# Gated delta attention with adaLN: triangular inverse built on 32 instead of 64 columns a unit, its dense factor transposed by VectorE and ScalarE instead of TensorE

## The chip, the cores and the metric

The kernel runs on one core of one Trainium2 chip, as one program. The metric is the device time of that core in microseconds. Before the change the median of 3 runs is 5353.44 us (5352.12 to 5354.04).

## The reference, cut to what matters

The whole computation is an adaLN block on x of 8 samples x 512 tokens x 256 channels: layer norm with modulation, a gated delta rule attention with 16 key heads and 32 value heads of width 128, a second layer norm, and a mixture of 2 of 6 small experts. Nearly all of the time lies in the attention, and the change lies in one part of it, the inverse of a unit lower triangular matrix:

```python
qkvz = hidden_states @ W_qkvz.T          # then a causal convolution of 4 taps and silu on q, k, v
q, k = l2norm(q) * dk ** -0.5, l2norm(k)
g = cumsum(g, chunk);  decay = tril(exp(g_i - g_j))
A = -strict_tril((k * beta) @ k.T * decay)          # one matrix for each head and chunk
T = solve_triangular(eye - A, eye, lower=True)      # the inverse of (I - A)
value_, k_cumdecay = T @ v_beta, T @ (k_beta * exp(g))
# then chunk by chunk, with a carried state:
v_new = value_ - k_cumdecay @ state
out   = (q * exp(g)) @ state + tril(q @ k.T * decay) @ v_new
state = state * exp(g_last) + (k * exp(g_last - g)).T @ v_new
```

The reference cuts the 512 tokens into chunks of 64; the kernel uses chunks of 128, which is the same recurrence. So one step of the kernel inverts 8 matrices of 128x128 ("units": 4 chunks x 2 value heads).

## The kernel before, in words

Three programs follow one another: `modulation_and_gates` (about the first 105 us), `attention`, and `experts` (about the last 170 us). `attention` walks over 128 steps, 8 samples x 16 key heads. A step works on one key head of one sample and its two value heads.

**How the order is fixed.** Each engine has its own list of tasks for one iteration (`PE_ORDER`, `ACT_ORDER`, `DVE_ORDER`, `POOL_ORDER`). A task is written `NAMEn@k`: the task NAME, its part n, of the step that lies k steps ahead of the iteration's own number. So an iteration works on up to four steps at once. Each engine executes its list strictly in that order; tasks of different engines are tied by semaphores, counted for each step (`counts`, and `t.wait(engine, name, k, back)`, where `back=1` means the step before). The loop body holds two iterations. SyncE issues the loads with its own list, `FEEDS`: pairs of a load and the number of steps that it runs ahead. A load whose wait is not met holds up all that stand behind it in the list.

**The tasks that matter here.**

- `P` (TensorE, 12 of them): the input projection, in two PSUM banks; `C` (ScalarE): its results copied and scaled; `T` (VectorE, 12): the taps of the convolution; `Z`, `SV`, `SQ`, `SK` (ScalarE): silu. `KT`, `QT`, `VT` transpose k, q, v on TensorE.
- `KK` (TensorE): k.T k and k.T q. `GL` (GpSimd), `GE` (ScalarE, behind a table load): the decay matrix `dec`. `GA` (VectorE, 8 instructions): `ga`, the scaled and decayed product. `SL` (GpSimd): its diagonal set to -1. `AD` (ScalarE): `a_d`, `ga` rounded to bf16. `AL` (GpSimd): the rest of the rounding, `a_lo`.
- The inverse by levels, in bf16, in one PSUM bank `p_lev` of 8 units x 64 columns. `AB` (VectorE): the two 64x64 diagonal blocks of each unit of `a_d` are copied into `a_bd`. `L` (TensorE): `a_bd` times an identity. `y0` (VectorE): the result times a mask. Then for n = 1 to 5: `M` (TensorE, `a_bd` times `y_h`), `q` (VectorE, times the level's mask, to `q_h`), `X` (VectorE, `y_h` transposed in 32x32 blocks to `x_t`), `XB` (ScalarE, the blocks of `x_t` copied to `x_bd`), `Y` (TensorE, `x_bd` times `q_h`), `y` (VectorE, added to `y_h`). Each of `L`, `M`, `Y` is 8 matmuls. After level 5 the 64x64 blocks are inverted.
- The join to 128: `s10`, `s11` (VectorE) copy `y_h` to the diagonal blocks of `y_dn`, the dense factor. `XD` (TensorE) transposes `y_dn` with 8 transpositions into `p_tr`, and `XD` (ScalarE) copies that to `x_dn`. `Q`, `p`, `Z`, `YC` (TensorE, VectorE, TensorE, ScalarE) make the lower left 64x64 block, `XC` (TensorE and ScalarE) its transpose.
- Two correction passes in higher precision: `D`, `d`, `N`, `n`, `E`, `e`, `W`, `IV` give `inv_t`.
- The recurrence over the 4 chunks: `TR`, `VW`, `U`, `ST`, `KS`, `RR`, `O`, `VX`, `SD`, `QD` (GpSimd, q times its decay, which `O1` to `O3` need). Then `OT`, `OQ`, `OS`, `OP`, `ON`, `HT`, `OY`, `YA`: the norm of the output and the output projection.

Where the tasks of one engine stand decides what waits. In the list of before GpSimd runs `GL@3 SL@2 SD1@1 QD@2`, ScalarE ends its list with `KT@3 XD@2 KN@3 YC@2 d0@2 d1@2 XC@2 GE@3` and begins it with `Z0@2 Z1@2 e0@1 IV0@1 AD@2 VX0@1`. VectorE begins with `VW0@1 AB0@2 AB1@2`. `FEEDS` begins with the weights, 3 steps ahead.

At the start of `attention`, GpSimd raises every semaphore by 3 steps' counts, clears `a_bd`, `x_bd`, `y_dn`, `pre` and `y_acc` and makes the small constants; the other engines wait for it (`init`).

Of the kernel before, what the change touches and what calls it, by code (L numbers as in the profile page):

```python
# [33 lines left out]
PE_ORDER = ("Z6@1 P9@2 D0@1 XC@1 D1@1 ON0@0 N0@1 ON1@0 P10@2 N1@1 KK0@2 KK1@2 P11@2 E0@1 P0@3 W0@1 E1@1 TR0@1 "  # L34
            "P1@3 U0@1 O0@1 L@2 W1@1 KS1@1 P2@3 M1@2 TR1@1 Y1@2 U1@1 O1@1 M2@2 P3@3 KS2@1 VT0@2 Y2@2 VT1@2 TR2@1 "
            "P4@3 M3@2 P5@3 U2@1 Y3@2 O2@1 M4@2 OY0@0 KS3@1 P6@3 Y4@2 TR3@1 QT@3 M5@2 O3@1 P7@3 Y5@2 P8@3 Q6@2 "
            "KT@3 XD@2 OY1@0")
ACT_ORDER = ("Z0@2 Z1@2 e0@1 IV0@1 AD@2 VX0@1 e1@1 SV1@2 OT0@1 C0@3 XB1@2 SV0@2 VX1@1 XB2@2 IV1@1 OT1@1 C1@3 OQ0@1 "
             "XB3@2 VX2@1 VK0@2 C2@3 VK1@2 OT2@1 XB4@2 OQ1@1 SQ@3 VX3@1 OQ2@1 XB5@2 OT3@1 OQ3@1 SK@3 QN@3 C3@3 "
             "KT@3 XD@2 KN@3 YC@2 d0@2 d1@2 XC@2 GE@3")  # L40
DVE_ORDER = ("VW0@1 AB0@2 AB1@2 T8@2 ST0@1 y0@2 X1@2 RR1@1 q1@2 VW1@1 y1@2 X2@2 ST1@1 q2@2 RR2@1 y2@2 X3@2 VW2@1 "
# [1566 lines left out]
```

## Time and profile before

| | |
|---|---|
| median of 3 runs | 5353.44 us |
| the profiled execution, its own time | 5352.04 us |
| its span in the trace | 5350.3 us |
| busy: TensorE matmul, weight load | 4982.9 us (93%), 3326.6 us (62%) |
| busy: VectorE, ScalarE, GpSimd | 4483.8 us (84%), 4371.8 us (82%), 2064.9 us (39%) |
| DMA queue of SyncE | 21.8% of 16 engines' span |
| mean granted TensorE clock | 0.987 of full |

The trace is one execution, recorded by the hardware. PE is TensorE's matmuls, PEld its weight loads (they overlap), DVE is VectorE, ACT ScalarE, POOL GpSimd, SP SyncE. Each line of a view names the line of the kernel (L911), the instruction, the tile that it writes, those that it reads, and shapes as partitions x elements. A start and a duration are in microseconds. In brackets stands how long the engine sat idle before, and who ended that. An engine's duration includes filling and draining, so the next instruction can start before the last has ended: the distance between two starts is the cost on the engine, the duration is what a reader of the result waits for.

### The profile page before, as it was taken

Reading aid. Unit: us, or ns where it says so; the run is one execution under the profiler, and the core shown is the slowest. Engines: PE = TensorE matmul, PEld = TensorE weight load, DVE = VectorE, ACT = ScalarE, POOL = GpSimd, SP = SyncE. Lnnn points to the kernel's source line nnn. Section 1 sums busy time; section 2 is a strip of 40 time slices with the busy share of each in tenths; the row PEclk is TensorE's granted clock in tenths of the full one; section 3 lists DMA queues with packets and bytes.
Section 4 is the critical chain, followed back from the end, with each engine's and each line's share of the span. In section 5 each row is a group of like instructions: output and inputs, shape, how many; then the busy total and the mean of one; then the engine's idle time right before and its main releaser. Section 6 shows DMA issues by size and latency. Waiting matters only on the chain. (4 is left out here: it accounts for less than half of the span.)

```text
span 5350.3 us, 132947 instructions
## 1 busy us (share of the span) xinstructions
PE 4982.9 (93%) x38788; PEld 3326.6 (62%) x38788; DVE 4483.8 (84%) x9152; ACT 4371.8 (82%) x9744; POOL 2064.9 (39%) x1433
## 2 busy tenths in 40 slices
PE   5899999999999999999999999999999999999978
PEld 3566666666666666666666666666666666666644
DVE  4888888888888888888888888888888888888853
ACT  3788888888888888888888888888888888888842
POOL 2344434344443434444344444434444343444410
PEclk7999999999999999999999999999999999999988
DMA  3222212121121212212121221212122121221112
GB/s 141 75 63 63 75 62 81 60 70 69 62 81 60 79 60 72 71 62 77 60 82 61 65 74 62 81 59 74 65 66 77 60 79 60 72 70 62 64 65 82
DMA packets 185165, 377.26 MB, mean 71 GB/s; under 512 B 86400, under 2 KB 95744, under 8 KB 184960
## 3 DMA queue, kind: packets, MB, share of 16 engines
q1 hardware_dynamic: 185088, 376.46, 21.8%
q14 instruction: 57, 0.47, 0.0%
q8 instruction: 20, 0.33, 0.0%
HBM read 360.13 MB, written 16.25 MB: 70 GB/s over the span
## 5 line engine op out<-in xcount | busy, mean ns | idle before, releaser
L653 PE MATMUL p_proj<-hid,w_in 128*128 128x512 f32 x3072 | 1620.5, 610 | 32.4 <-POOL ident L1163 29.7
L998 DVE SCALAR_TENSOR_TENSOR conv<-pre,taps,conv 128x512 f32<-128x512 f32 x1536 | 1207.8, 793 | 41.9 <-ACT conv L857 37.6
L911 ACT ACTIVATE x_bd<-x_t 64x512 bf16<-64x512 bf16 x1280 | 804.5, 629 | 215.7 <-DVE x_t L1079 198.9
L1205 POOL TENSOR_TENSOR o_sc<-o_sc,neg_half 128x8 f32<-128x8 f32 x128 | 268.6, 2099 | 1622.0 <-DVE o_sc L1135 1622.0
L653 PEld LDWEIGHTS p_proj<-hid,w_in 128*128 128x128 f32 x3072 | 496.6, 192 | 64.5 <-POOL ident L1163 30.0
L838 PE MATMUL p_out<-h_t,w_out 128*128 128x512 f32 x1024 | 501.9, 613 | 0.8 <-DVE h_t L1140 0.8
L1072 DVE TENSOR_TENSOR y_h<-p_lev,y_h 128x512 bf16<-128x512 f32 x640 | 441.3, 690 | 44.2 <-PE p_lev L707 37.9
L1116 DVE TENSOR_TENSOR vw<-p_b,w_c 128x256 f32<-128x256 f32 x384 | 156.9, 409 | 378.8 <-PE p_b L796 378.8
L1079 DVE STREAM_TRANSPOSE x_t<-y_h 128x512 bf16<-128x512 bf16 x640 | 454.6, 710 | 19.3
L1064 DVE TENSOR_TENSOR q_h<-p_lev,consts 128x512 bf16<-128x512 f32 x640 | 438.6, 685 | 37.9 <-PE p_lev L701 33.3
L1172 POOL TENSOR_TENSOR low<-g_row,consts 128x1024 f32<-128x1024 f32 x128 | 302.1, 2360 | 410.1 <-ACT dec L895 409.9
L1200 POOL TENSOR_TENSOR state_dec<-state,g_exp 128x256 f32<-128x256 f32 x256 | 157.3, 615 | 764.5 <-DVE state L1123 501.9
L1051 DVE SCALAR_TENSOR_TENSOR ga<-p_out,neg_c,dec 128x256 f32<-128x256 f32 x1024 | 413.0, 476 | 23.3 <-PE p_out L677 15.3
L818 PE MATMUL p_b<-vx,ga 128*128 128x128 f32 x2048 | 374.8, 275 | 0.0
L707 PEld LDWEIGHTS p_lev<-q_h,x_bd 128*128 128x128 bf16 x5120 | 219.4, 98 | 240.1 <-ACT x_bd L911 176.4
L857 ACT ACTIVATE conv<-p_proj,taps 128x512 f32<-128x512 f32 x512 | 353.2, 690 | 1.6
L856 ACT ACTIVATE pre<-p_proj 128x512 f32<-128x512 f32 x512 | 305.5, 597 | 32.1 <-PE p_proj L653 32.0
L817 PE MATMUL p_b<-state,q_dec 128*128 128x128 f32 x1536 | 324.0, 293 | 0.5 <-ACT vx L960 0.5
L1193 POOL TENSOR_TENSOR q_dec<-kq,e_row 128x512 f32<-128x512 f32 x256 | 320.5, 1274 | 0.0
L701 PEld LDWEIGHTS p_lev<-y_h,a_bd 128*128 128x128 bf16 x5120 | 223.3, 98 | 156.1 <-issue 144.3
L895 ACT ACTIVATE dec<-low,g_neg 128x128 f32<-128x128 f32 x1024 | 313.2, 388 | 1.5
L1105 DVE SCALAR_TENSOR_TENSOR rr<-p_a,g_exp,v_tok 128x128 f32<-128x128 f32 x768 | 228.3, 339 | 101.6 <-PE p_a L783 101.6
(210 smaller groups left out, 12168.4 us busy)
## 6 DMA issues: line engine op xcount, KB each, us to landing
w_in<-in_w_in SPq DMA_DIRECT2D x128, 768.0 KB, 6.2
g_row<-rows_scratch SPq DMA_DIRECT2D x128, 512.0 KB, 3.1
hid<-h_scratch SPq DMA_DIRECT2D x128, 512.0 KB, 7.3
e_row<-exp_rows_scratch SPq DMA_DIRECT2D x128, 512.0 KB, 5.1
w_out<-in_w_out SPq DMA_DIRECT2D x128, 256.5 KB, 2.6
x<-in_x SPq DMA_DIRECT2D x8, 512.0 KB, 10.4
h_scratch<-x SPq DMA_DIRECT2D x8, 512.0 KB, 2.6
y_scratch<-y_acc SPq DMA_DIRECT2D x8, 512.0 KB, 5.6
```

The lines of the kernel that those rows point to most:

```text
L653: last = pe.matmul(p_proj[tile % 2][:], w_in[p][:, kt, tile * P:(tile + 1) * P], hid[p][:, kt, :], start=(kt == 0), stop=(kt == KT - 1))
L817: pe.matmul(p_b[:, at], q_dec[p][:, n, h, :], state[n % 2][:, h, :], start=True, stop=False)
L818: last = pe.matmul(p_b[:, at], ga[p][:, n * HD + h, 1, :], vx[:, h, :], start=(n == 0), stop=True)
L838: last = pe.matmul(p_out[n][:], w_out[p][:, h * D + n * P:h * D + (n + 1) * P], h_t[:, :, h, :], start=(h == 0), stop=(h == HD - 1))
L857: act.activation(conv[:, n, :], p_proj[n % 2][:], ACT.Copy, scale=taps[p][:, n, PAD:PAD + 1])\
L911: last = act.activation(x_bd[block, :, block], x_t[block], ACT.Copy)
L998: dve.scalar_tensor_tensor(conv[:, tile, :], pre[:, tile, j:j + S], taps[p][:, tile, j:j + 1], conv[:, tile, :], ALU.mult, ALU.add).then_i ...
L1051: last = dve.scalar_tensor_tensor(ga[p][:, u], kk, neg_c[p][:, n, h:h + 1], each(dec[:, u, :], 2), ALU.mult, ALU.mult)
L1064: dve.tensor_tensor(q_h[:], levels(), each(const["mask"][:, n * HB:(n + 1) * HB], U), ALU.mult)\
L1072: dve.tensor_tensor(y_h[:], levels(), y_h[:], ALU.add).then_inc(s["y_done"], 1)
L1079: dve.transpose(x_t[:].rearrange("p u f -> p (u f)"), y_h[:].rearrange("p u f -> p (u f)"))\
L1193: last = pool.tensor_tensor(q_dec[p][:, :, h, :], kq[p][:, :, 1, :], e_row[p][:].rearrange("p (c h) i -> p c h i", h=HD)[:, :, h, :], ALU. ...
```

## The change

The levels run on 32 columns a unit: the four 32x32 diagonal blocks of each unit are inverted by levels, so `p_lev` is used on 8 x 32 columns, and the masked levels are one fewer. The join from 32 to 64 is the last `M`/`Y` pair, with the off-diagonal blocks `a_off` in place of `a_bd` and no mask. The dense factor's transpose no longer passes through TensorE: its diagonal 32x32 blocks are copied by ScalarE from `x_t` (which `X5` made), the two off-diagonal blocks are transposed by VectorE (`XE`). The lists of all engines and `FEEDS` are new, and so is the start of `attention`.

```diff
-LEVELS = 6
+LEVELS = 5
+PE_ORDER = ("P11@2 E0@1 P0@3 W0@1 E1@1 TR0@1 P1@3 U0@1 P2@3 L@2 O0@1 KS1@1 M1@2 P3@3 TR1@1 W1@1 Y1@2 P4@3 M2@2 "
+            "U1@1 O1@1 Y2@2 P5@3 KS2@1 P6@3 VT0@2 M3@2 TR2@1 VT1@2 Y3@2 U2@1 O2@1 M4@2 P7@3 KS3@1 Y4@2 OY0@0 M5@2 "
+            "TR3@1 P8@3 QT@3 Y5@2 O3@1 KT@3 Q6@2 OY1@0 Z6@2 P9@3 XC@2 D0@2 D1@2 P10@3 ON0@1 ON1@1 N0@2 N1@2 KK0@3 "
+            "KK1@3")
+ACT_ORDER = ("Z0@2 SV1@2 Z1@2 e0@1 IV0@1 AD@2 VX0@1 e1@1 C0@3 OT0@1 XB1@2 C1@3 OQ0@1 VX1@1 XB2@2 IV1@1 SV0@2 OT1@1 "
+             "C2@3 XB3@2 OQ1@1 VX2@1 VK0@2 XB4@2 VK1@2 SQ@3 OT2@1 SK@3 XB5@2 VX3@1 C3@3 OQ2@1 QN@3 OT3@1 OQ3@1 "
+             "XD@2 KN@3 YC@2 KT@3 d0@2 XC@2 d1@2 GE@3")
+DVE_ORDER = ("HT0@0 HT1@0 SM0@2 n0@1 SM1@2 SM2@2 SM3@2 n1@1 GA0@2 GA1@2 GA2@2 GA3@2 T7@2 T8@2 VW0@1 AB0@2 AB1@2 "
+             "AB2@2 AB3@2 ST0@1 y0@2 X1@2 RR1@1 q1@2 VW1@1 y1@2 X2@2 T3@3 AB4@2 q2@2 T0@3 ST1@1 y2@2 T4@3 X3@2 "
+             "RR2@1 SN1@2 T1@3 q3@2 VW2@1 y3@2 X4@2 T5@3 ST2@1 q4@2 T2@3 RR3@1 y4@2 AB5@2 X5@2 T6@3 YA0@0 q5@2 "
+             "s8@2 s9@2 s10@2 s11@2 YD0@2 SN0@2 XE0@2 YD1@2 XE1@2 OS0@1 OS1@1 p6@2 SN2@2 T9@3 T10@3 YA1@0 KN@3 "
+             "QN@3 T11@3")
+POOL_ORDER = ("OP@0 ON@0 PW@2 GL@3 QD@1 SL@2 SD1@1 AL@2 SD2@1")
...
-            FEEDS = ((weights, 3), (gate_cols, 3), (out_weights, 1), (gate_exps, 1), (rows, 4),
-                     (tap_rows, 3), (gate_rows, 3))
+            FEEDS = ((gate_cols, 3), (weights, 3), (tap_rows, 3), (rows, 3), (gate_exps, 1),
+                     (gate_rows, 1), (out_weights, 0))
...
                 elif name == "M":
                     t.wait(pe, "y_done", n)
+                    if n == 5:
+                        t.wait(pe, "abd")
+                    rows = a_off if n == 5 else a_bd
                     for u in range(U):
-                        last = pe.matmul(p_lev[:, u * HB:(u + 1) * HB], a_bd[:, u, :], y_h[:, u, :], start=True, stop=True)
+                        last = pe.matmul(p_lev[:, u * QB:(u + 1) * QB], rows[:, u, :], y_h[:, u, :], start=True, stop=True)
...
-                elif name == "XD":
-                    t.wait(pe, "ydn")
-                    t.wait(pe, "x12", back=1)
-                    for u in range(U):
-                        last = pe.transpose(p_tr_h[:, u * P:(u + 1) * P], y_dn[:, u, :], ident_h[:])
-                    last.then_inc(s["xt6"], 1)
...
-                    for block in (slice(0, HB), slice(HB, P)):
-                        last = act.activation(x_bd[block, :, block], x_t[block], ACT.Copy)
+                    for block in range(4):
+                        last = act.activation(x_bd[part(block), :, part(block)], x_t[part(block)], ACT.Copy)
...
                 elif name == "XD":
-                    t.wait(act, "xt6")
+                    t.wait(act, "xt_done")
                     t.wait(act, "w_mm", back=1)
-                    act.activation(x_dn[:].rearrange("p u i -> p (u i)"), p_tr_h, ACT.Copy).then_inc(s["xdn"], 1)
+                    for block in range(4):
+                        last = act.activation(x_dn[part(block), :, part(block)], x_t[part(block)], ACT.Copy)
+                    last.then_inc(s["xdn"], 1)
...
-                    dve.tensor_copy(a_bd[half(n), :, half(n)], a_d[half(n), :, half(n)]).then_inc(s["abd"], 1)
+                    if n < 4:
+                        dve.tensor_copy(a_bd[part(n), :, part(n)], a_d[part(n), :, part(n)]).then_inc(s["abd"], 1)
+                    else:
+                        j, i = part((n - 4) * 2), part((n - 4) * 2 + 1)
+                        dve.tensor_copy(a_off[j, :, i], a_d[j, :, i]).then_inc(s["abd"], 1)
...
+                elif name == "YD":
+                    t.wait(dve, "y_mm", 5)
+                    i, j = part(n * 2 + 1), part(n * 2)
+                    dve.tensor_copy(y_dn[i, :, j], levels()[i]).then_inc(s["ydn"], 1)
+                elif name == "XE":
+                    t.wait(dve, "ydn", 5 + n)
+                    i, j = part(n * 2 + 1), part(n * 2)
+                    dve.transpose(x_dn[j, :, i], y_dn[i, :, j]).then_inc(s["xe"], 1)
...
-            for name, counted in s.items():
-                pool.sem_inc(counted, SPARE * counts[name])
-            for tile in (a_bd, x_bd, y_dn):
-                pool.memset(tile[:], 0.0)
+            spare(pool, "rooted g_low strict alo q_dec_done sdec opow o_nrm")
```

`part(n)` is the n-th slice of 32 (`QB`), `HB` is 64. `s8` to `s11` copy the four diagonal blocks into `y_dn`, in place of two copies; `y5` is gone, `YD0` and `YD1` take its result straight from `p_lev`. `spare` raises the semaphores that an engine signals on that engine itself; VectorE now clears the tiles (`a_off` and `x_dn` among them) and of `pre` only the padding; and TensorE's first projection no longer waits for `init`, only `L` of the first step does. `Q` reads `y_dn` in place of `y_h`.

## Rows read from the trace of the kernel before

**Rows 1.** Windows, steady stretch: length, busy of PE, PEld, DVE, ACT, POOL, clock, DMA, GB/s.

```profile
2000.00:3000.00 1000.00, 951.57 (x7604) 639.83 (x7603) 870.56 (x1795) 855.79 (x1921) 408.45 (x281) 1.00 0.22 68
```

**Rows 2.** GpSimd's `OP`, one a step: count, durations (ns), first and last start.

```profile
L1205 POOL TENSOR_TENSOR o_sc<-o_sc,neg_half x125: 2082/2106/2109, 249.4 to 5095.8; 128x8 f32<-128x8 f32 x125
```

**Rows 3.** Waits of ScalarE, window 2000:4000: us in total, times, longest.

```profile
ACT x_bd L911 <- DVE x_t L1079: 76.1, 102, 1.3
ACT f L947 <- PE p_out L750: 67.7, 102, 1.1
ACT inv_t L943 <- PE p_out L778: 49.7, 51, 1.0
```

**Rows 4.** Timeline of TensorE: start, us, what, idle before.

```profile
3005.54 0.40 PE L701 MATMUL p_lev<-y_h,a_bd 128*128 128x64 bf16 x8
3005.77 0.69 PE L796 MATMUL p_b<-rr,inv_t 128*128 128x128 f32 x4
...
3024.25 0.61 PE L713 MATMUL p_tr<-ident_h,y_dn 128*128 128x128 bf16 x8
3024.70 1.94 PE L838 MATMUL p_out<-h_t,w_out 128*128 128x512 f32 x4
...
3031.28 0.40 PE L760 MATMUL p_out<-f,x_dn 128*128 128x128 bf16 x4 [1.15 <-DVE h_t L1140]
```

**Rows 5.** Groups of instructions, all of the span: count, busy us, mean ns, idle before.

```profile
L911 ACT ACTIVATE x_bd<-x_t 64x512 bf16<-64x512 bf16 x1280 | 804.5, 629 | 215.7 <-DVE x_t L1079 198.9
...
L1079 DVE STREAM_TRANSPOSE x_t<-y_h 128x512 bf16<-128x512 bf16 x640 | 454.6, 710 | 19.3
L1072 DVE TENSOR_TENSOR y_h<-p_lev,y_h 128x512 bf16<-128x512 f32 x640 | 441.3, 690 | 44.2 <-PE p_lev L707 37.9
...
L1057 DVE COPY a_bd<-a_d 64x512 bf16<-64x512 bf16 x256 | 73.4, 287 | 6.4 <-ACT a_d L903 2.4
...
L1123 DVE COPY state<-p_a 128x256 f32<-128x256 f32 x128 | 53.4, 418 | 0.8 <-PE p_a L806 0.8
```

**Rows 6.** Timeline of ScalarE, one iteration.

```profile
3005.21 1.27 ACT L911 ACTIVATE x_bd<-x_t 64x512 bf16<-64x512 bf16 x2 [0.21 <-DVE x_t L1079]
3006.50 0.63 ACT L878 ACTIVATE v_t<-conv 128x512 f32<-128x512 f32 x1
...
3025.50 1.04 ACT L916 ACTIVATE x_dn<-p_tr 128x1024 bf16<-128x1024 bf16 x1
3026.40 0.62 ACT L882 ACTIVATE squares<-p_out 128x512 f32<-128x512 f32 x1
3027.08 0.59 ACT L922 ACTIVATE y_dn<-p_lev 64x512 bf16<-64x512 f32 x1
...
3029.69 0.60 ACT L947 ACTIVATE f<-p_out 128x512 bf16<-128x512 f32 x1 [0.32 <-PE p_out L750]
...
3032.07 2.44 ACT L895 ACTIVATE dec<-low,g_neg 128x128 f32<-128x128 f32 x8
...
3039.81 1.05 ACT L903 ACTIVATE a_d<-ga 128x1024 bf16<-128x1024 f32 x1
...
3044.72 1.27 ACT L911 ACTIVATE x_bd<-x_t 64x512 bf16<-64x512 bf16 x2 [0.35 <-DVE x_t L1079]
```

**Rows 7.** Timeline of GpSimd.

```profile
3004.48 2.51 POOL L1193 TENSOR_TENSOR q_dec<-kq,e_row 128x512 f32<-128x512 f32 x2
...
3034.66 2.36 POOL L1172 TENSOR_TENSOR low<-g_row,consts 128x1024 f32<-128x1024 f32 x1 [3.27 <-ACT dec L895]
3038.11 1.10 POOL L1181 TENSOR_SCALAR_AFFINE_SELECT ga<-ga 128x1024 f32<-128x1024 f32 x1 [1.09 <-DVE ga L1051]
```

**Rows 8.** DMA issues on the page: count, KB each, us to landing.

```profile
hid<-h_scratch SPq DMA_DIRECT2D x128, 512.0 KB, 7.3
```

**Rows 9.** Timeline of the start of attention.

```profile
111.28 0.95 POOL L1156 MEMSET a_bd<- 128x1024 bf16 x1 [46.24 <-issue]
...
117.81 8.51 PE L653 MATMUL p_proj<-hid,w_in 128*128 128x512 f32 x14 [29.73 <-POOL ident L1163]
```

More of the change, by code:

```diff
@@ L33 @@
 PAD = TAPS - 1
[L34 to L41, printed above, removed]
[3 rows of a table removed]
-POOL_ORDER = ("OP@0 ON@0 PW@2 GL@3 SL@2 SD1@1 QD@2 SD2@1 AL@2")
+PE_ORDER = ("P11@2 E0@1 P0@3 W0@1 E1@1 TR0@1 P1@3 U0@1 P2@3 L@2 O0@1 KS1@1 M1@2 P3@3 TR1@1 W1@1 Y1@2 P4@3 M2@2 "
[6 more added lines that the diff above has]
+DVE_ORDER = ("HT0@0 HT1@0 SM0@2 n0@1 SM1@2 SM2@2 SM3@2 n1@1 GA0@2 GA1@2 GA2@2 GA3@2 T7@2 T8@2 VW0@1 AB0@2 AB1@2 "
[4 rows of a table added]
+POOL_ORDER = ("OP@0 ON@0 PW@2 GL@3 QD@1 SL@2 SD1@1 AL@2 SD2@1")
 def const_columns():
-    return [("ident", P), ("mean", P), ("ones", P), ("tri", P), ("bound", CH), ("eye", HB), ("mask", LEVELS * HB),
+    return [("ident", P), ("mean", P), ("ones", P), ("tri", P), ("bound", CH), ("eye", QB), ("mask", LEVELS * QB),
             ("upper", P), ("lower", P)]
@@ L692, in emit @@
                 elif name == "L":
-                    t.wait(pe, "abd")
+                    if isinstance(t.number, int) and t.number == 0:
+                        pe.wait_ge(init, 2)
+                    t.wait(pe, "abd", 4)
                     t.wait(pe, "y21", back=1)
                     for u in range(U):
-                        last = pe.matmul(p_lev[:, u * HB:(u + 1) * HB], a_bd[:, u, :], eye_h[:], start=True, stop=True)
+                        last = pe.matmul(p_lev[:, u * QB:(u + 1) * QB], a_bd[:, u, :], eye_h[:], start=True, stop=True)
                     last.then_inc(s["q_mm"], 1)
@@ L719, in emit @@
                     for u in range(U):
-                        last = pe.matmul(p_lev[HB:P, u * HB:(u + 1) * HB], a_d[0:HB, u, HB:P], y_h[0:HB, u, :],
+                        last = pe.matmul(p_lev[HB:P, u * HB:(u + 1) * HB], a_d[0:HB, u, HB:P], y_dn[0:HB, u, 0:HB],
                                          start=True, stop=True)
@@ L732, in emit @@
                     t.wait(pe, "y21")
-                    t.wait(pe, "xdn")
+                    t.wait(pe, "x12", back=1)
                     pe.sem_inc(passed, 1)
@@ L981, in _ @@
         def _(dve):
[L982 to L985 removed]
+            for tile in (a_bd, a_off, x_bd, y_dn, x_dn, y_acc):
+                dve.memset(tile[:], 0.0)
+            dve.memset(pre[:, :, 0:PAD], 0.0).then_inc(init, 1)
+            spare(dve, "tap0 tap1 tap2 tap3 xe k_sum q_sum scaled w_scaled q_scaled ga_done abd q_done y_done xt_done ydn p6_done "
+                       "n_done rr_done vw_done st_done osm h_done y_added")
+            dve.wait_ge(init, 2)
             def levels():
[L988 removed]
+                return p_lev[:, 0:U * QB].rearrange("p (u f) -> p u f", f=QB)
             def emit(name, t, n):
@@ L1076, in emit @@
                         t.wait(dve, "xbd", back=1)
+                        t.wait(dve, "xdn", back=1)
                     else:
```

70 lines of the change are left out of this document (41 added, 29 removed), and 3 rows, old and new, of the table DVE_ORDER.

## The prediction

> **What bounds the kernel now.** I read the windows first. In the steady stretch of 1000 us TensorE's matmuls are busy 951.6 us, VectorE 870.6, ScalarE 855.8, GpSimd 408.5, at the full clock (1.00, the 2.4 GHz level), and DMA takes 22% [rows 1]. The reader is to see three engines within a tenth of each other: none can be called the bound by its share alone. Next, one task that occurs once a step gives the period: 125 starts of `OP` from 249.4 to 5095.8 us, so (5095.8 - 249.4) / 124 = 39.08 us [rows 2]. In units of one period TensorE is busy 37.2 us, VectorE 34.0, ScalarE 33.5. Some 126 steps run at this pace; the rest is the two other stages, filling and draining.
>
> Then the waits and the timelines, for what each engine's idle time hangs on. TensorE's longest gap is `N0`, 1.15 us behind `HT0` [rows 4], and `HT0` stands behind taps in VectorE's list: in that part VectorE runs without a gap, so VectorE is what binds there. ScalarE idles 5.6 us a period; the two largest pieces are `XB` waiting for the transpose `X` (76.1 us over 51 periods, 1.5 us each) and `d` waiting for `D` (1.3 us), then `IV0` for `W0` (1.0 us) [rows 3]. So the kernel now is bound by a loop over engines in which VectorE has the least slack, TensorE little, and ScalarE 5.6 us. What matters is who gives work and who gets it.
>
> **The change, part by part, for one step.**
>
> *TensorE.* The eight transpositions go: from 3024.25 to the next start at 3024.70, 0.45 us [rows 4]. The levels stay 11 tasks of 8 matmuls. One such task of 64 columns takes 3005.77 - 3005.54 = 0.23 us, 29 ns a matmul, each with its own weight load of 128 columns. With 32 columns I bound it by half (0.12 us a task, 1.2 us a step) and by no gain; each matmul still loads all its weights, so I take no gain. A new wait arises where `ON0`, `ON1`, `N0`, `N1`, `KK0` now follow each other. TensorE needs 36.7 us.
>
> *VectorE.* Work on `p_lev` halves from 512 to 256 elements: 0.69 us becomes 0.42, the duration of the 128x256 copy out of PSUM [rows 5]. That is 10 such instructions (5 `q`, `y0` to `y4`), -2.7 us; `y5` goes, -0.7. `X` scales in the same way, 0.71 to 0.44, five of them, -1.35. Against this: six `AB` copies for two and four `s` copies for two. Two of 64x512 take 0.29 us each plus a gap of 0.03; a block of half the elements I put at 0.24, so +1.2. `YD` twice 0.45, `XE` twice 0.47: +1.85. In sum -1.7 us: VectorE goes from 34.0 to 32.3 us, and `T7`, `T8` (1.4 us) move into its idle time before `VW0`. VectorE is relieved.
>
> *ScalarE.* It pays. `XB` is 2 instructions of 64x512 at 0.629 us [rows 5]; the pair starts at 3005.21 and the next instruction at 3006.50, so it costs 1.29 us, no overlap at either seam [rows 6]. An element costs (1.05 - 0.63) / 512 = 0.82 ns, from the 1024 element copy `AD` and the 512 element silu in the same rows, so 256 elements save 0.21 us and one 32x256 copy takes 0.42, with the gap 0.44. Bounds: 0.32, if it overlaps its successor by 0.10 as 128-partition instructions do (`x_dn` lasts 1.04 us, its successor starts 0.90 after it [rows 6]), and 0.63, if a block cost as much as a larger one. I take 0.44, since the nearest rows are those of the same copy on part of the partitions. `XB`: 5 x (4 x 0.44 - 1.29) = +2.35 us. `XD`: 4 x 0.44 = 1.76 for 0.90, +0.86. ScalarE gets +3.2 us: 33.5 becomes 36.7 of 39.1, and only 2.4 us may be left for all its waits if the period is to stay. Its list is now the tightest loop, so I walk it.
>
> - *From `XB1` to `YC`.* Now 3027.08 - 3005.21 = 21.9 us [rows 6]. Add 3.2; `KT` (0.5) moves behind `YC`; the wait of `XB2` (1.3 of the 1.5) goes, because the level chain gets shorter (`y` and `X` -0.27 each) and more work stands between the `XB`; of small waits I take off another 0.7. 22.6 us.
> - *From `YC` to `d1`.* Now 2.61 us (3027.08 to 3029.69). `XC`, on 64 partitions as `YC` with its 0.59, moves between `d0` and `d1`, +0.6; `d1` no longer idles, -0.32; on TensorE `XC` goes ahead of `D0`, which I put at +0.15. `KT` fills a part of the wait for `D0` and costs nothing. 3.05 us.
> - *From `d1` to the next `XB1`.* Now 15.0 (3029.69 to 3044.72). `d1`, table load and `GE` take 4.2 (`XC` stood between and is gone). Then GpSimd: `GL` cannot start before `GE` is done (its own `low` is read until then) and takes 2.36. Behind it now stands `QD@1`, 2.51 us, ahead of `SL@2`, 1.10 [rows 7]. With hand-overs 6.3, so `AD` starts 10.5 after `d1`. `AD` 1.05, four `AB` 1.0, `L` 0.6, `y0` 0.45, `X1` 0.5 with hand-overs of 0.05: 14.15 us.
>
> 22.6 + 3.05 + 14.15 = 39.8; hand-overs may be a tenth too generous, so I take 39.7 for 39.08: +0.62 us x 126 = +78 us. In this walk `QD` before `SL` costs about 0.9 us of it: `IV0` would be done 9.6 after `d1`, and `AD` waits, with `VX0`, `e1` and `C0` queued behind it on ScalarE, for which `VW1`, `W1` and `T0` wait in turn.
>
> The Trainium skill ("ScalarE: Activation LUTs", section "What ACT_TABLE_LOAD costs") says that back-to-back ACTIVATEs overlap by about 93 ns. By that rule the four copies would cost what two cost now. This case agrees for 128 partitions (0.90 between starts of 1.04) and does not for 64 (1.29 for two of 0.63).
>
> *The loads.* All nine loads of a step now stand behind `gate_cols`, which waits for `SN0` in the last fifth of VectorE's list. The weights land 7.3 us after issue [rows 8]; I estimate some 12 us of listed work between `SN0` and `P0`, and some 13 until `QD` needs `e_row`. Hidden, but no longer by much: cost 0, or up to 1 us a step if late.
>
> *The start.* GpSimd's first clearing is at 111.28 and the first projection at 117.81 [rows 9]. These 6.5 us, which TensorE waited for, go; what gates it next is the landing of its first loads. Between -6.5 and 0 I take -4 us.
>
> **The sum.** 5352.0 (the profiled execution's own time, 1.7 over its span) + 78 - 4 = 5426; the median of runs is 1.4 above that execution: 5427 us.
>
> **Rivals.**
>
> *Copies on 32 partitions overlap.* Then a copy costs 0.32, `XB` nothing more than now, ScalarE's loop falls by 24 x 0.12 = 2.9 to 36.8, and TensorE binds: 36.7 us plus the waits around `N` and `KK`, about 37.8 in all. -1.3 x 126 - 4 = -168: 5185. For it: 128-partition instructions overlap; against it: no 64-partition one does. It decides below a seam of about 0.41 us a copy.
>
> *VectorE was the bound, and ScalarE's waits give way.* My walk keeps 2.9 us of waits on ScalarE. If `QD` ran in a gap before `GL`'s release, or `IV0` and `d0` waited half as long because VectorE arrives earlier, the period would be 38.7: -0.4 x 126 - 4 = -54: 5299. For it: the 1.15 us at `N0` and VectorE's gapless part; against it: these waits hang on TensorE and GpSimd, which get no shorter.
>
> *Gain and cost cancel*: within 0.1 us a step, 5350.
>
> *The loads come late.* One trigger for 2.5 MB; if `P0` or `QD` waited 1 us each step on top of the forecast: 5427 + 126 = 5550. Against it: 22% DMA share.
>
> *The narrower levels do nothing on TensorE*: that is in the forecast already; its other end is -1.2 us of TensorE's work, which pays only if TensorE binds.
>
> **Chances.** About 0.2% (10 us) is what a measurement of this kernel can tell from no change. Forecast 0.50 (its own range 5370 to 5490); overlap 0.10; waits give way 0.26; cancel 0.06; loads late 0.08. Slower 0.58, faster 0.36, same 0.06. The range 5235 to 5500 leaves out most of the overlap case and of the late loads.
>
> **What would show it.** Busy time of ScalarE in a steady window from 856 to about 920 per 1000; `x_bd` near 0.42 us with 0.44 between starts; a period near 39.7; `a_d` waiting about 0.9 us for GpSimd's `ga`; `x_bd`'s waits near zero; VectorE's share falling to about 815, TensorE's matmuls to about 925. The forecast is wrong if the seam between 32-partition copies is below 0.4, or if ScalarE's waits sum to less than 2.4 us a step, or if the first wait of `P0` is a DMA.

## The result: 5909 us for a forecast of 5427

The changed kernel takes 5909.0 us (median of 4 runs, 5908.1 to 5913.1) beside 5352.9 us for the kernel before: a ratio of 1.104, 95% interval 1.1021 to 1.1059. The sign was forecast as likelier than not; the size was not: 5909 lies far above the range 5235 to 5500.

### The profile after

The steady stretch of [rows 1], in the same columns:

```profile
2000.00:3000.00 1000.00, 883.58 (x6655) 579.42 (x6655) 791.62 (x1813) 825.86 (x2013) 367.71 (x253) 0.95 0.18 62
```

Every engine is less busy than before, ScalarE too, and the granted clock has fallen from 1.00 to 0.95 of full speed. Nothing got fuller: there is a new hole. Over a full 90 periods a step took 43.72 us for 39.09 (starts of `a_d`), and not evenly: steps alternate between 41.8 and 45.6 us. A loop turn holds two steps, so the hole comes once a turn. The waits, window 2000:4000 (us in total, times, longest), name it:

```profile
ACT z_t L876 <- PE p_proj L665: 141.5, 23, 7.1
...
PEld p_out L773 <- issue: 100.5, 92, 4.5
```

23 times in 46 steps ScalarE's `z_t` waits for a projection, 6.2 us on average and 7.1 at most; before, no wait of ScalarE was over 1.3 us [rows 3]. The timelines of one such place, VectorE first (start, duration, what, idle before):

```profile
3006.79 0.87 DVE L1015 SCALAR_TENSOR_TENSOR conv<-pre,taps,conv 128x512 f32<-128x512 f32 x1
3010.93 1.41 DVE L1178 SCALAR_TENSOR_TENSOR h_t<-p_out,norm_w,z_t 128x512 f32<-128x512 f32 x2 [3.27 <-issue]
3012.26 2.09 DVE L1030 TENSOR_SCALAR neg_n<-root 128x8 f32<-128x8 f32 x1
...
3015.67 1.12 DVE L1042 SCALAR_TENSOR_TENSOR neg_c<-cc,inv 128x8 f32<-128x8 f32 x1
3016.71 0.68 DVE L1131 SCALAR_TENSOR_TENSOR y<-y_dn,p_out 128x512 f32<-128x512 bf16 x1
3017.50 1.66 DVE L1068 SCALAR_TENSOR_TENSOR ga<-p_out,neg_c,dec 128x256 f32<-128x256 f32 x4
```

then TensorE and ScalarE:

```profile
3011.83 1.24 PE L773 MATMUL p_out<-f,x_dn 128*128 128x128 bf16 x8 [2.99 <-DVE h_t L1178]
3015.08 2.04 PE L689 MATMUL p_out<-kq 128*128 128x256 f32 x4 [2.01 <-DVE y L1131]
3017.53 2.05 PE L689 MATMUL p_out<-kq 128*128 128x256 f32 x4 [0.41 <-DVE y L1131]
```

```profile
3013.14 0.60 ACT L876 ACTIVATE z_t<-p_proj 128x512 f32<-128x512 f32 x1
3013.63 0.62 ACT L892 ACTIVATE v_t<-conv 128x512 f32<-128x512 f32 x1
3021.32 0.60 ACT L876 ACTIVATE z_t<-p_proj 128x512 f32<-128x512 f32 x1 [7.07 <-PE p_proj L665]
```

`T11` is the last entry of the new VectorE list and `HT0` its first: the idle time stands exactly at the branch back. It is put down to "issue", that is, to nothing that a semaphore shows, and small instructions behind it (`neg_n` over 8 columns, 2.09 us) are slow as well. TensorE waits 2.99 us for `HT0` and then 2.01 for `y`, and the windows of that stretch show its clock (third-last column the granted clock, then the DMA share):

```profile
3005.00:3010.00 5.00, 3.76 (x35) 2.41 (x34) 2.66 (x4) 4.05 (x8) 3.94 (x2) 1.00 0.94 338
3010.00:3014.00 4.00, 1.17 (x8) 0.69 (x8) 3.07 (x3) 3.97 (x10) 2.03 (x1) 0.66 0.27 111
3014.00:3020.00 6.00, 4.51 (x9) 3.02 (x10) 5.18 (x11) 0.26 (x1) 2.76 (x3) 0.50 0.00 1
```

Behind the idle time the clock is 0.50, the 1.2 GHz level, and four matmuls of `KK` take 2.04 us. `P11` stands behind `KK` in TensorE's list, hence the 7.07 us of ScalarE.

The cause shows in the page's list of DMA queues (packets, MB, share). The kernel before has 57 packets on queue 14; after:

```profile
q14 instruction: 364, 2.98, 0.2%
```

These packets of 8192 bytes carry instructions. Over the whole loop they come 5.6 a turn, before 0.6. So part of some engine's loop is loaded anew in each turn, which I call a refetch. The queue does not say for which engine; the idle time at VectorE's branch points to VectorE, and experiment 5, which changes VectorE's program alone, confirms it. Which bodies are loaded anew, and what it costs, had to be found.

### The profile page after: what moved, and what is told of

Same layout as the page of the kernel before. It is cut to its first block and busy times, and to the rows that moved or that the text cites. A ratio compares the mean times of both kernels' runs of the same rounds, so it can differ in the third digit from the quotient of the medians.

```text
span 5911.3 us, 135338 instructions
## 1 busy us (share of the span) xinstructions
PE 5151.8 (87%) x37764; PEld 3349.3 (57%) x37764; DVE 4553.1 (77%) x10311; ACT 4703.8 (80%) x11408; POOL 2067.7 (35%) x1428
## 5 line engine op out<-in xcount | busy, mean ns | idle before, releaser
L665 PE MATMUL p_proj<-hid,w_in 128*128 128x512 f32 x3072 | 1682.4, 631 | 25.8 <-DMA hid<-h_scratch 23.1
L925 ACT ACTIVATE x_bd<-x_t 32x256 bf16<-32x256 bf16 x2560 | 1053.2, 411 | 48.0 <-DVE x_t L1104 16.0
L1238 POOL TENSOR_TENSOR o_sc<-o_sc,neg_half 128x8 f32<-128x8 f32 x128 | 210.9, 1648 | 1901.0 <-DVE o_sc L1173 1901.0
L689 PE MATMUL p_out<-kq 128*128 128x256 f32 x1024 | 387.0, 515 | 149.1 <-DVE y L1131 146.9
L876 ACT ACTIVATE z_t<-p_proj 128x512 f32<-128x512 f32 x256 | 152.4, 595 | 375.2 <-PE p_proj L665 370.8
L689 PEld LDWEIGHTS p_out<-kq 128*128 128x128 f32 x1024 | 228.3, 247 | 265.5 <-issue 237.9
L1178 DVE SCALAR_TENSOR_TENSOR h_t<-p_out,norm_w,z_t 128x512 f32<-128x512 f32 x256 | 180.6, 747 | 244.8 <-issue 174.6
L783 PEld LDWEIGHTS p_out<-y,ga 128*128 128x128 f32 x2048 | 279.1, 207 | 122.5 <-issue 119.8
L1096 DVE TENSOR_TENSOR y_h<-p_lev,y_h 128x256 bf16<-128x256 f32 x512 | 216.3, 422 | 169.4 <-PE p_lev L724 169.4
L783 PE MATMUL p_out<-y,ga 128*128 128x128 f32 x2048 | 301.7, 294 | 15.4 <-DVE ga L1068 15.1
```

The costliest lines, as they stand in the source:

```text
L665: last = pe.matmul(p_proj[tile % 2][:], w_in[p][:, kt, tile * P:(tile + 1) * P], hid[p][:, kt, :], start=(kt == 0), stop=(kt == KT - 1))
L689: last = pe.matmul(p_out[n][:, c * 2 * P:(c + 1) * 2 * P], kq[p][:, n * 2 + c, 0, :], kq[p][:, n * 2 + c].rearrange("p a i -> p (a i)"), s ...
L783: last = pe.matmul(bank(n)[:, u - n * 4, :], ga[p][:, u, 0, :], y1[:, u, :], start=True, stop=True)
L925: last = act.activation(x_bd[part(block), :, part(block)], x_t[part(block)], ACT.Copy)
```

## The experiments

The theory at the start was length: VectorE's loop had grown from 286 to 336 records a turn. Its rival was place: the loop's edge had moved from before `VW0`, where VectorE waits for TensorE anyway, to before `HT0`, on which TensorE waits. A record here is one instruction in the trace, waits and branches included. Experiments 2, 4, 8, 14 and 15 were timed once, the others at least four times.

**1. Fewer waits.** In `AB`, `s`, `YD` the waits that an earlier task of the list has already passed are asked only once (306 records a turn).

```
- t.wait(dve, "ad"); t.wait(dve, "q_mm", back=1)
+ if n == 0: t.wait(dve, "ad"); t.wait(dve, "q_mm", back=1)
  (s and YD alike)
```

> The changed kernel with 18 repeated waits a step taken out of VectorE's program (AB1 to AB5, s9 to s11, YD0, YD1 wait for nothing that AB0, s8 did not wait for already); every instruction, its order and all tiles are the same. Theory F (fetch): VectorE's loop body of 336 recorded instructions no longer stays on the chip, so it is fetched again at each turn of the loop (260 instruction DMA packets between 1000 and 5000 us, 33 before), and the turn costs 6.3 us on a chain with HT0. With some 300 instructions the fetches should be back near 33, the alternation 40.6 / 46.9 us should become about 40.6 / 41.1, and the time about 5911 - 63 x 5.8 = 5545 us. Theory S (ScalarE): the step is long because of the narrower copies; then the waits change nothing: 5880 to 5910.

Measured 5915.2 us, ratio 1.1055 (1.1037 to 1.1074), still 5.6 packets and 5 us above the rival's range. So 306 records are not short enough, if it is the length that counts.

**2. The edge moved.** The entries from `HT0@0` to `T8@2` go to the end of VectorE's list, with their offsets raised by one; the order of the work is the same.

```
- DVE_ORDER = ("HT0@0 ... T8@2 VW0@1 ... T11@3")
+ DVE_ORDER = ("VW0@1 ... T11@3 HT0@1 ... T8@3")
```

> The changed kernel with VectorE's list rotated: the same tasks in the same order, but the loop's edge stands before VW0, where VectorE waits for TensorE anyway, instead of before HT0. Theory F: the refetch stays (about 260 packets) but some 2.4 us of the 3.3 us at the edge fall into VectorE's own wait, and the slow instructions behind the edge are no longer on the chain HT0, n0, KK: 5911 - 63 x 3 to 4 = 5660 to 5720 us. If the place of the edge does not matter, and only the fetch itself (contention) does: 5890 to 5910.

Measured 5565.6 us beside 5352.0, with 59 packets in all. Less than expected, and for a reason that neither theory had: the packets were gone, though the body was no shorter (337).

**3. Both.** Experiments 1 and 2 together.

> Both: fewer waits and the edge before VW0. Theory F: no refetch, and the edge hidden: 5500 to 5550 us, up to 0.5 us a turn (30 us in all) below the kernel with fewer waits alone. What is left over 5353 is the price of the change itself: 1.2 to 1.5 us a step, where the prediction walked to 0.6.

Measured 5660.9 us, ratio 1.058 (1.0562 to 1.0597): a shorter loop, and the packets back. A miss that helped most, for it left only where the body lies.

**4. The kernel before, padded** with 25 repeated waits in front of its `VW`, body 311.

```
+ if n == 0:
+     for _ in range(25): t.wait(dve, "w_scaled")
```

> The kernel before, with one wait that is long met repeated 25 times a step in VectorE's program right before VW0, where VectorE idles 3.2 us: the loop body grows from 286 to 336 or more instructions. Theory F: fetches appear at each turn (over 200 packets in 4000 us) and the time rises by 60 to 250 us though no work was added: 5410 to 5600 us. If the loop body's size does not matter: 5350 to 5375 us (the waits themselves, 25 x 0.06 = 1.5 us, fit into the idle time).

Measured 5387.4 us, below the 5410 to 5600 expected, with 5.6 packets a turn: the kernel before can be brought into the same state.

From these I put up the theory that holds to the end. Number each engine's records in the order of the trace, from 0, and add a constant; a block begins at every multiple of 128. A body that touches three blocks stays; one that touches four is fetched anew each turn. The constant is fitted for each engine: 61 to 70 for VectorE (65 below), 69 to 83 for ScalarE (76 below). The size of 128 was a guess from the packets of 8192 bytes.

```
kernel                  engine   first  length  blocks  packets a turn
before                  VectorE   257    286      3       0.6
after                   VectorE   298    336      4       5.6
1 fewer waits           VectorE   283    306      4       5.6
2 edge moved            VectorE   328    337      3       0.6
3 both                  VectorE   313    307      4       5.6
4 before padded         VectorE   269    311      4       5.6
5 after, 40 fillers     VectorE   337    336      3       0.6
6 before, 45 fillers    VectorE   302    286      4       5.6
14 after, 12 fillers    VectorE   309    336      4       5.6
15 after, 90 fillers    VectorE   387    336      4       5.6
8 half of the copies    ScalarE   295    292      4       5.6
9 the same, 45 fillers  ScalarE   340    292      3       0.6
```

The first six rows served to fit it; 5, 6, 14 and 15 were predicted. Row 8 came unannounced and fixed ScalarE's constant; 9 was predicted from it. All seventeen kept traces agree, those of the experiments below included. Other sizes can be tried on them: of blocks of 16 to 699 records, with any number of them staying, VectorE's bodies allow only 116 to 132 records with three staying. ScalarE has one refetched body and allows many sizes, so there 128 is carried over from VectorE.

**5. The changed kernel with 40 fillers**, semaphore increments that nobody waits for, on VectorE ahead of its loop. The loop is untouched.

```
+ for _ in range(40):
+     dve.sem_inc(passed, 1)
```

> The changed kernel with 40 empty increments put into VectorE's program before its loop (done at the start of attention, while VectorE idles). The loop itself is unchanged: 336 recorded instructions, edge before HT0. Theory A (place in memory): an 8 KB instruction packet holds 128 instructions; a loop that touches three such blocks stays on the chip, one that touches four is fetched again at every turn. Five kernels fit this if the blocks' edge lies 61 to 70 instructions off the count of recorded ones: refetched are the bodies that start at 298, 283, 313, 269 (lengths 336, 306, 307, 311), not those at 257 and 328 (286 and 337). Starting at 338 this body fits into three blocks: no refetch (about 0.6 packets a turn instead of 5.6) and 5545 to 5580 us. Theory B (length of the body): 5911 and 5.6 packets a turn, as before.

Measured 5564.2 us, ratio 1.0401 (1.0383 to 1.0418). As expected, with 59 packets in all: 40 instructions that do nothing, executed once, take 341 us off ((5909.0 - 5352.9) - (5564.2 - 5349.0)). The same place of the timeline, `T11` to `GA0`, from this kernel:

```profile
3033.34 0.78 DVE L1017 SCALAR_TENSOR_TENSOR conv<-pre,taps,conv 128x512 f32<-128x512 f32 x1
3034.86 1.41 DVE L1180 SCALAR_TENSOR_TENSOR h_t<-p_out,norm_w,z_t 128x512 f32<-128x512 f32 x2 [0.75 <-PE p_out L840]
3036.18 0.16 DVE L1032 TENSOR_SCALAR neg_n<-root 128x8 f32<-128x8 f32 x1
...
3038.57 3.23 DVE L1070 SCALAR_TENSOR_TENSOR ga<-p_out,neg_c,dec 128x256 f32<-128x256 f32 x8 [0.52 <-ACT dec L909]
```

```profile
3037.08 2.22 PE L689 MATMUL p_out<-kq 128*128 128x256 f32 x8 [0.28 <-DVE y L1133]
```

From `T11` to `GA0` now 38.57 - 33.34 = 5.23 us; in the changed kernel 17.50 - 6.79 = 10.71. The 5.48 us between, once a turn, times some 63 turns are 345 us, as much as the 341. Eight matmuls of `KK` take 2.22 us where four took 2.04.

Experiments 2 and 5 have the loop's edge in different places and no refetch, and lie within 2 us of each other. So the edge before `HT0` costs nothing by itself; it costs only together with a refetch.

**6. The kernel before with 45 fillers** ahead of VectorE's loop.

> The kernel before with 45 empty increments before VectorE's loop; body of 286 unchanged, edge before VW0, start 302 instead of 257. Theory A: it now touches four blocks, 5.6 packets a turn, and costs what the refetch costs with the edge at VectorE's idle place: 5370 to 5390 us. Theory B: 5353 and 0.6 packets a turn.

Measured 5494.0 us, ratio 1.0273 (1.0256 to 1.029). The packets came as predicted; the price did not (145 us for 20 to 40). VectorE's waits in this kernel, window 2000:4000 (us in total, times, longest), show where it arises:

```profile
DVE vw L1118 <- PE p_b L796: 144.3, 72, 3.2
DVE state L1125 <- issue: 38.1, 22, 2.5
```

The wait before `VW0` is as long as before and does hide the load at the branch. A second idle time, 1.7 us in 22 of 25 turns and put down to "issue", stands one tap behind `VW0`, ahead of `ST0`, on which the recurrence waits. It makes up most of the 2.3 us a turn that the kernel lost; experiment 4, with its 25 waits ahead of `VW0`, has none there. Experiment 3 against 2 gives 95 us for that edge, experiment 4 35. So the price seems to go by where in the list the code runs out; what sets that was not tried.

**14, 15. Twelve fillers and ninety.** They tell the theory of place from "any filler helps".

> The changed kernel with 12 one-instruction fillers on VectorE ahead of its loop, the loop untouched; its body starts at about record 310. Theory, what decides is where the body lies in blocks of 128 instructions: 12 are too few, the body of 336 still touches a fourth block, 5.6 packets a turn and 5890 to 5920 us. Rival, any fillers ahead of the loop help (more time for the first pass to be loaded, or code elsewhere): under 5700 us.

> As before with 90 fillers for 12; the body starts at about record 388. Theory of blocks: 40 fillers brought the body into three blocks, 90 carry its end over the next edge again: 5.6 packets a turn return and the time is 5890 to 5920 us. Rival, past some number of fillers it stays good: 5555 to 5575 us.

Measured 5931.6 and 5885.6 us, 12 above and 4 below the range given, with 364 packets each. 12 fillers are too few, 40 right, 90 too many: the refetch goes by the place and comes back with the next edge.

The second question is what the change costs without any of this: 215 us, 1.7 us a step, for 0.62 forecast.

**7. Selection first.** Experiment 2 with GpSimd's `SL@2` ahead of `QD@1`.

> The changed kernel with the edge before VW0 (5565.6 us, no refetch) and GpSimd's SL ahead of QD instead of behind it. Theory P (the prediction's walk): a_d waits 1.7 us a step for GpSimd; that wait goes, and 1.0 to 1.7 us a step come back: 5350 to 5440 us. Rival Q: O1, which needs QD, takes over, or ScalarE's copies alone make the step: 5520 to 5565 us.

Measured 5503.8 us, ratio 1.0288 (1.0271 to 1.0305): 62 us less, between the two ranges and half of the least that the theory gave. The means over some hundred steps show where the rest went: from `d1` to `AD` 9.59 us for 11.41, but from `AD` to `XB1` 4.95 for 3.65. The wait of `a_d` is gone, and `VX0` behind it now waits for `VW0` (28.1 us in 50 steps; in experiment 2 that wait is too small to be listed). In this kernel `SL` takes 1.45 us, for 1.10 before [rows 7].

**8. Half of the copies.** Experiment 2 with the copies of blocks 2 and 3 in each `XB` left out.

```
- for block in range(4):
+ for block in range(2):
```

> The changed kernel with the edge before VW0, with two of the four copies of each XB left out (the blocks 2 and 3 of x_bd stay zero). That takes 10 x 0.42 = 4.2 us a step from ScalarE. Theory C (ScalarE's list is the bound of the step): 1.5 to 3 us a step come back, 5190 to 5380 us, until TensorE binds. If ScalarE is not the bound but the chain GE, GL, QD, SL, AD: under 0.5 us a step, 5500 to 5565 us.

Measured 5343.7 us, as expected: ten copies of 0.42 us less, 4.2 us a step, give 222 us, and a period of 39.20 us for 40.88, 1.7 a step. ScalarE's list does bear on the period, but only two fifths of what is taken off it reach the time. ScalarE's own loop, shorter now, had 5.6 packets a turn.

**9. The same with 45 fillers on ScalarE.**

> As the half-copies kernel (copies of blocks 2 and 3 of x_bd left out, so part of the product is not computed; 5343.7 us), with 45 one-instruction fillers on ScalarE ahead of its loop and the loop itself untouched. Theory of position: the refetch of 5.6 packets a turn that ScalarE's loop showed there goes (its body then starts at about record 340 instead of 295 and touches three blocks of 128 instructions), and the time is 5290 to 5340 us, since ScalarE then waits less at its turn. Rival 1, the length of the loop or the number of instructions sets the refetch: the packets stay and the time is 5340 to 5355 us. Rival 2, ScalarE's refetch lies beside a wait anyway: packets gone, time within 5 us of 5343.7.

Measured 5328.3 us, ratio 0.9965 (0.995 to 0.9979), as expected, with the packets gone: 13 us less than experiment 8 when each is measured against the kernel before, near the edge of what can be told (the kernel of experiment 8 was timed once). The theory of place held for ScalarE too in this one pair, and its refetch cost little there. Since half of a product is missing, this is no version to use.

**10. The kernel before with its copies split.** Each `XB` as four copies of 64x256 for two of 64x512.

```
- last = act.activation(x_bd[block, :, block], x_t[block], ACT.Copy)
+ for us in (slice(0, U // 2), slice(U // 2, U)):
+     last = act.activation(x_bd[block, us, block], x_t[block, us], ACT.Copy)
```

> The kernel before with each ScalarE copy into x_bd split in two along the units, four copies of 64x256 a round for two of 64x512, the data the same; 45 fillers ahead of ScalarE's loop so that the longer loop is not refetched. The two added copies a round are priced at about 0.23 us each over what they replace, some 2.3 us of ScalarE a step, and nothing else changes. Theory, ScalarE's list and the chain through its copies carry the period: 0.3 to 1.5 us a step, 5390 to 5540 us. Rival, VectorE or TensorE carries it and ScalarE has slack: 5345 to 5365 us.

Measured 5416.4 us, ratio 1.013 (1.0113 to 1.0147), in the range: 70 us, 0.55 a step. The added ScalarE time is less than the 2.3 us that were priced:

```profile
3004.79 1.45 ACT L914 ACTIVATE x_bd<-x_t 64x256 bf16<-64x256 bf16 x4 [0.34 <-DVE x_t L1082]
3006.26 0.63 ACT L880 ACTIVATE v_t<-conv 128x512 f32<-128x512 f32 x1
L914 ACT ACTIVATE x_bd<-x_t 64x256 bf16<-64x256 bf16 x1007 | 362.4, 407 | 75.0 <-DVE x_t L1082 70.7
```

Four copies and the next start are 1.47 us apart where two took 1.29 [rows 6], so a step gets 0.9 us of ScalarE, and six tenths of it reach the time. The copy of 64x256 lasts as long as the one of 32x256, 407 and 411 ns: it is priced by its columns, not by its partitions. But four of them fit into 1.45 us: the second copy onto the same 64 partitions starts 321 ns after the first, the one onto the other 64 partitions 413 ns after its predecessor (medians over 503 rounds). The four copies of the changed kernel all go to different partitions and never overlap.

**11. Copies shared.** Experiment 7 with GpSimd making blocks 2 and 3 in rounds 2 to 5.

```
- POOL_ORDER = ("... AL@2 SD2@1")
+ POOL_ORDER = ("... AL@2 SD2@1 XP2@2 XP3@2 XP4@2 XP5@2")
+ elif name == "XP":
+     t.wait(pool, "xt_done", n)
+     ...
+     for block in (2, 3):
+         last = pool.tensor_copy(x_bd[part(block), :, part(block)], x_t[part(block)])
```

> The rotated kernel with the selection first (5503.8 us), the copies of blocks 2 and 3 of x_bd in rounds 2 to 5 made by GpSimd at the same time as ScalarE makes blocks 0 and 1; ScalarE's list loses 8 copies of 0.42 us, 3.4 us a step. 45 fillers ahead of ScalarE's loop. Theory, ScalarE's list and the round through its four copies carry the period (leaving out 10 of 20 copies gave 222 us): 5330 to 5430 us. Rival 1, GpSimd's pair of copies takes longer than ScalarE's four did, each round is later by over 0.3 us: 5500 to 5650 us. Rival 2, GpSimd's copies slow VectorE beside them as VectorE's taps slow GpSimd: 5430 to 5500 us.

Measured 5783.3 us, ratio 1.0815 (1.0797 to 1.0833), above every range given. Timelines of GpSimd and of ScalarE:

```profile
3001.36 0.61 POOL L1247 TENSOR_TENSOR state_dec<-state,g_exp 128x256 f32<-128x256 f32 x1 [3.72 <-DVE state L1168]
3002.30 0.83 POOL L1231 COPY x_bd<-x_t 32x256 bf16<-32x256 bf16 x2 [0.33 <-POOL state_dec L1247]
3005.28 0.83 POOL L1231 COPY x_bd<-x_t 32x256 bf16<-32x256 bf16 x2 [2.15 <-DVE x_t L1107]
```

```profile
2999.60 0.83 ACT L925 ACTIVATE x_bd<-x_t 32x256 bf16<-32x256 bf16 x2
```

A pair on GpSimd takes 0.83 us, as long as ScalarE's. But the pair of round 2 stands in GpSimd's list behind `SD2`, which waits for VectorE's `state` until 3001.36, and starts 2.7 us after ScalarE's: TensorE has its blocks at 3003.1, where four copies on ScalarE would have been done 1.7 us after 2999.60. TensorE idles 2.3 us there, and its granted clock is at the half level in each step behind it (0.96 on average over the steady stretch, for 1.00 in experiment 7):

```profile
3003.23 0.38 PE L722 MATMUL p_lev<-q_h,x_bd 128*128 128x32 bf16 x8 [2.32 <-issue]
```

```profile
3003.20:3006.20 3.00, 2.97 (x13) 1.78 (x14) 1.44 (x3) 0.66 (x2) 0.79 (x2) 0.50 0.00 0
```

The 1.8 us and the slower matmuls behind them are most of the rise of the period from 40.37 to 42.67. The miss is one of placing; whether sharing pays with the pair ahead of `SD2` was not tried.

**12. Taps earlier.** Experiment 7 with `T7` and `T8` ahead of `HT0` instead of behind `GA3`.

> The rotated kernel with the selection first (5503.8 us), and VectorE's two taps T7 and T8 put ahead of HT0 instead of behind GA3, so that they no longer lie beside GpSimd's selection and decay products. Theory, VectorE's two-input work beside them slows GpSimd: the selection goes from 1.45 us back to about 1.1, the two products from 2.94 to about 2.55; the way from the selection to ScalarE's a_d gets 0.3 us shorter, while HT0 and what follows may start up to 1.5 us later: 5450 to 5560 us, most likely 5490. Rival, the selection is slow for its place after ga or for what TensorE and ScalarE do: durations unchanged, 1.45 and 2.94.

Measured 5571.9 us, ratio 1.0422 (1.0404 to 1.0439), somewhat above its range and 68 us above experiment 7; the durations came out as the theory had them. GpSimd in this kernel, no VectorE taps beside it:

```profile
3005.20 1.10 POOL L1210 TENSOR_SCALAR_AFFINE_SELECT ga<-ga 128x1024 f32<-128x1024 f32 x1 [2.03 <-DVE ga L1064]
3006.26 2.51 POOL L1222 TENSOR_TENSOR q_dec<-kq,e_row 128x512 f32<-128x512 f32 x2
```

against experiment 2, with the taps beside it (3042.48 to 3045.1 on VectorE):

```profile
3041.59 2.97 POOL L1222 TENSOR_TENSOR q_dec<-kq,e_row 128x512 f32<-128x512 f32 x2
3044.51 1.55 POOL L1210 TENSOR_SCALAR_AFFINE_SELECT ga<-ga 128x1024 f32<-128x1024 f32 x1
```

and experiment 2's VectorE there:

```profile
3042.48 2.63 DVE L1011 SCALAR_TENSOR_TENSOR conv<-pre,taps,conv 128x512 f32<-128x512 f32 x2
```

Both lose: `QD` 0.46 us, `SL` 0.45, and the two taps take 2.63 us where `T9` and `T10` take 1.53. The Trainium skill has this in "GPSIMD Engine Reference", section "Specifications": GpSimd's SBUF interfaces are shared with VectorE and contended by VectorE instructions that read two SBUF inputs, as the taps do. The trace agrees, and puts 18% on `QD` and 41% on `SL` to it.

The time rose all the same, because `HT0` now comes later: TensorE waits 63.7 us for `h_t` in the window 2000:4000, for 31.5 in experiment 7, and once a turn its clock falls to 0.50 behind that wait (0.98 on average). The eight matmuls of `KK` take 3.26 us there, for 2.22 in experiment 5.

**13. Tiny taps.** Experiment 2 with `T7` and `T8` cut to one column.

```
+ w = 1 if n in (7, 8) else S
```

> The kernel with the moved edge (5565.6 us), with VectorE's taps T7 and T8 cut to one column each, so that two of twelve steps of the convolution are left out for all other columns. GpSimd's QD and SL then have no two-input work of VectorE beside them, and nothing is put in another place. Theory, their slowing (2.96 for 2.51 and 1.45 for 1.10 us) is what the way from d1 to the next XB1 was too short by in the forecast: both go back, a_d starts 0.8 us earlier a step, 5445 to 5490 us. Rival, the round through ScalarE's copies has slack there and the time is given back later: durations back, time 5530 to 5570 us.

Measured 5454.2 us, ratio 1.0199 (1.0182 to 1.0216). As expected. The same rows of GpSimd and, behind them, of ScalarE:

```profile
3014.45 2.51 POOL L1223 TENSOR_TENSOR q_dec<-kq,e_row 128x512 f32<-128x512 f32 x2
3016.91 1.10 POOL L1211 TENSOR_SCALAR_AFFINE_SELECT ga<-ga 128x1024 f32<-128x1024 f32 x1
```

```profile
3007.65 0.59 ACT L958 ACTIVATE f<-p_out 128x512 bf16<-128x512 f32 x1
3018.26 1.06 ACT L913 ACTIVATE a_d<-ga 128x1024 bf16<-128x1024 f32 x1 [0.86 <-POOL ga L1211]
```

From `d1` to `AD` 18.26 - 7.65 = 10.61 us, the next time 10.39. The forecast had 10.5.

The cut taps also take 1.0 us a step of work from VectorE, which would be a rival. Experiment 2 speaks against it: there VectorE, past the taps, waits 0.6 us for TensorE ahead of `VW0` and then 1.4 us a step for `a_d`, so a VectorE that is ready sooner would only wait longer.

```profile
DVE a_bd L1071 <- ACT a_d L913: 69.4, 49, 1.5
```

## Why the prediction was wrong

Above the kernel before, the change costs 556 us where 74 were forecast (78 of the steps, -4 of the start). The 556 split by runs into 341 (experiment 5), 109 (215 of experiment 5 less 106 of experiment 13) and 106.

*The step that failed most is the part on VectorE.* "The change, part by part" summed VectorE's instructions and found it "relieved"; the loading of its code, at the loop's edge, stood in the sum at nothing and without a reason. The runs showed 341 us for it. The part never asked where the list's edge had gone or where the longer loop lies. The diff shows the first: `HT0@0` at the head of the list, which in the kernel before stood in its last quarter, and whose wait at `N0` the first part names as TensorE's longest gap [rows 4]. That the body would fall across a fourth block, and that this has a price, could not be read from the trace of before; that a delay right before `HT0` would be paid in full could. 341 of the 482 us missed are here: 5.5 us a turn, half of it at the branch (4.14 us from `T11` to `HT0` for 1.52), half as slow instructions and TensorE at the half clock behind it.

*From `d1` to the next `XB1`*, forecast 14.15. Experiment 2, which has the changed kernel's work without the refetch, shows it in ScalarE's timeline:

```profile
3008.98 1.69 ACT L921 ACTIVATE x_bd<-x_t 32x256 bf16<-32x256 bf16 x4 [0.21 <-DVE x_t L1100]
3012.73 1.67 ACT L921 ACTIVATE x_bd<-x_t 32x256 bf16<-32x256 bf16 x4
3014.43 0.60 ACT L954 ACTIVATE inv_t<-p_out 128x512 f32<-128x512 f32 x1
...
3031.71 0.59 ACT L933 ACTIVATE y_dn<-p_lev 64x512 bf16<-64x512 f32 x1
...
3034.79 0.58 ACT L958 ACTIVATE f<-p_out 128x512 bf16<-128x512 f32 x1
...
3046.09 1.06 ACT L913 ACTIVATE a_d<-ga 128x1024 bf16<-128x1024 f32 x1 [1.66 <-POOL ga L1210]
3049.57 1.69 ACT L921 ACTIVATE x_bd<-x_t 32x256 bf16<-32x256 bf16 x4
```

`d1` to `AD` takes 11.30 us for 10.5, because `QD` and `SL` were priced at 2.51 and 1.10 [rows 7], durations from a place with no tap beside them, while the same change puts `T7` and `T8` there. The way on to `XB1` takes 3.48 here and 3.83 a step earlier, for 3.65. Over 101 steps the means are 11.41 from `d1` to `AD` and 3.65 on to `XB1`, 15.06 us in all. This is the second mis-sized term, 0.9 us a step; experiment 13 takes the taps' work away, comes to 10.50 from `d1` to `AD`, and gets 0.88 a step back (111 us over 126 steps). The forecast wait of `a_d` for `ga`, 0.9 us, is 1.7 in experiment 2 and 0.8 in experiment 13.

*From `XB1` to `YC`*, forecast 22.6: 3031.71 - 3008.98 = 22.73. *From `YC` to `d1`*, forecast 3.05: 3.08. Both right.

*The seam*, forecast 0.44 us a copy: four copies and the next start at 3014.43 - 3012.73 = 1.70, 0.425 a copy. The first rival, that these copies overlap, fell: a copy of 411 ns is followed 425 ns later. That overlap belongs to full 128 partitions, as the prediction's reading of the rows had it, is too narrow: in experiment 10 copies onto 64 partitions overlap when the next one goes to the same 64. ScalarE is busy 36.0 us a step in experiment 2 (1759.35 us per 2000) for 36.7 forecast; half of the difference is the seam (24 copies of 0.015).

*The sum.* 22.73 + 3.08 + 11.41 + 3.65 gives 40.87 us, the measured period of 40.88 but for rounding. I had taken 39.8 down to 39.7 for generous hand-overs; there were none. Without the contention, experiment 13's period is 39.99 for 39.7, and 0.29 x 126 = 37 us is about the 32 by which it stands over the forecast.

*TensorE.* No gain was taken for 32 columns. A task of 8 matmuls took 0.20 to 0.21 us for 0.23 [rows 4], some 0.3 us a step off an engine that does not bind: right.

*VectorE.* Forecast 32.3 us a step. In experiment 2 it is busy 1637.44 us per 2000, 33.5 at 40.88 us. Of the 1.2 us more, 0.5 are its twelve taps, mean 834 ns for 792, slowed while GpSimd works beside them as GpSimd is by them; the rest was not broken down.

*The loads.* No `P0` waited for a DMA behind the first one, so the rival of late loads fell. *The start*, forecast -4 us within -6.5 and 0: the first projection starts at 115.03 for 117.81 [rows 9], -2.8.

*VectorE as the bound, ScalarE's waits giving way.* The period did not fall, so as a forecast it failed; but ScalarE's waits do give way in part: of 4.2 us taken from ScalarE only 1.7 came through, and of 0.9 us added to the kernel before 0.55. A walk along one engine overstates what each edit there is worth, though its sum was good.

No version of the change that was run beats the kernel before with the computation whole. The nearest is experiment 7 at 1.029. Moving `T7` and `T8` to a place beside neither GpSimd's `QD` and `SL` nor `HT0`, together with experiment 7, was not tried.

## What to carry to other kernels

Where a change touches the list of a looped engine, count instruction packets on the page before and after, and look at what stands at the branch back: here an idle time put down to "issue" there, once a turn, was code being loaded. Some tens of idle instructions ahead of the loop tell whether it is the place, and can mend it (40 did, 12 and 90 did not). Putting the edge where the engine waits anyway lowers the price of a refetch, from 341 us to between 35 and 145 here, and does not remove it. And a duration taken from a row holds only beside the neighbours it had there: when a change moves VectorE's two-input work beside GpSimd's, price both again.
